# Decoder layer of attention, cross mixing and experts: a piece copy moved from ScalarE to GpSimd, batched small columns and inverse deviations, and new instruction orders in the attention

## The chip, the cores and the metric

One core of a Trainium2 chip runs the whole program in one launch. The metric is the device time of that core in microseconds (us); the runs before have a median of 232.91.

## The reference

The input x is 16 batches of 128 rows by 128 columns, ctx the same. Three sublayers follow one another, each closed by a layer norm of x plus its result:

```python
x = _layernorm(x + attention(x, w_qkv, w_out, b_out))        # 16 heads of 8, rotary positions, softmax
x = _layernorm(x + cross(x, ctx, ctx, Wq, bq, Wout, bout))   # FFT correlation, mean over batch and head, top 11 lags, rolls of v
x = _layernorm(x + experts(x, Wg, bg, W1, b1, W2, b2, gamma, beta))  # 8 experts of width 256, 2 chosen per row
```

All is float32. The change touches the first sublayer and what the kernel computes beside it.

## The kernel before, in words

Each engine has its own list of steps, written out one call after another, and semaphores order them between engines; an engine never looks past a step that waits. So the order of the calls in each engine's block is the schedule.

**The attention, batch by batch (n = 0 to 15).** TensorE: `qkv(n)` multiplies x by the projections (L965, with 8 cross columns of x and, L966, 8 of ctx). ScalarE: `keep_qkv(n)` copies it to SBUF (L706). Rotary positions: `rope_products` (L432, L438) and `rope_sum` (L444), on VectorE for batches 0 and 1 and on GpSimd from 2 on; the result is `qk`. For float32 accuracy from bf16 matmuls, q and k are split into three bf16 pieces laid side by side in `stack` (two buffers): `first_piece` (ScalarE, L719) writes the highest piece; `remainder` (VectorE for 0 and 1, then GpSimd, L450) writes `rest`, what it leaves; `second_piece` (ScalarE, L723) and `second_copy` (ScalarE, L727) both round `rest` into `stack`, at two places of it, since the middle piece stands twice on each side; `third_piece` (GpSimd, L456) writes the lowest. `k_transposes(n)` on TensorE turns the k half (L1003), `kT_copy(n)` on ScalarE keeps it (L732). The q half is turned by TensorE for batches 0 to 2 and by SyncE's `q_transpose(n)`, a DMA transpose (L341), from 3 on.

`scores(n, u)`, u = 0 and 1 (L981): 8 matmuls into `score_pair`; `maxima(n, u)` on VectorE (L1383) reduces them to row maxima, `pieces_of_maxima` (L463, L465) splits these, `maxima_transpose(n)` on TensorE (L1028) turns them, `mT_copy(n)` on ScalarE (L745) keeps them and `spread_maxima(n)` in SyncE's queue sends them by two DMAs (L348) into rows of `qT`, so that `scoresT(n, u)` (L997) has the transposed scores less their maxima. `softmax_exp(n, u)` on ScalarE (L737) makes the probabilities; `weighted(n, u)` (L1042, L1046) multiplies v and ones by them. VectorE: `reciprocal` (L1394) and `divide` (L1399); TensorE: `project(n)` (L1059); VectorE: `residual_sum` (L1406), `statistics_of_rows`, `mean_and_variance`, `normal_rows` (L469), for which GpSimd gives the inverse deviation (L493 an addition, L496 a power of -0.5). `residual(g)` (L1413) adds the output bias to four batches of x.

SyncE's queue issues, in order, `spread_maxima(n)`, a background load (among them the expert weights w1 and w2, from n = 6 on), `q_transpose(n + 3)`, and so on; `q_transpose(n)` waits for `third_piece(n)` and `second_copy(n)`.

**Around the loop.** For k = 8 to 15 every list is a loop whose body handles several batches at once, shifted: TensorE has `scoresT(k-6, 0)`, `scores(k-4, 0)`, `qkv(k)`, `project(k-7)`, `scoresT(k-6, 1)`, `scores(k-4, 1)`, the two halves of `weighted(k-6)`, `k_transposes(k-2)`, `maxima_transpose(k-4)`. Ahead of it a start and behind it a drain are written out. `keep_clock(i)` is i matmuls whose result nobody reads (L945, L951), where TensorE would wait.

**Beside and behind the attention.** `w1_high_piece(i)` on ScalarE (L702) and `w1_low_piece(i)` on GpSimd (L521), i = 0 to 3, split the expert weights into two parts each. Behind the last exponential, ScalarE loads a function table, runs `key_spectrum` and takes the last deviation (L846). VectorE then makes products of spectra (L1561), and `part` and `lag` by two TENSOR_SCALAR and two SCALAR_TENSOR_TENSOR (L1565 to L1571), whose inputs are in SBUF. These go through a matmul, a top 11 and a softmax, in series, before the cross result. GpSimd's `add_cross_bias(g)` (L601) works on four batches each. The experts, from about 114 us to the end, are not touched.

## Time and profile before

| what | us |
|---|---|
| median of 3 runs | 232.91 |
| lowest, highest | 232.44, 234.08 |
| profiled execution, span from its first to its last instruction | 229.2 |
| TensorE busy in it | 215.3 (94%) |
| VectorE | 181.3 (79%) |
| ScalarE | 142.5 (62%) |
| GpSimd | 111.6 (49%) |

The page gives no whole time for the profiled execution, only its span; what lies around the span is in the runs' times alone. A row of a timeline gives start and duration in us; `x8` is the number of instructions merged in it, and a bracket the idle time of the engine before it and what ended that. PE is TensorE's matmuls, PEld its weight loads, DVE VectorE, ACT ScalarE, POOL GpSimd, SPq SyncE's DMA issues. The granted clock of TensorE is 0.991 of full speed on the mean over the span, and 1.00 throughout the attention.

### The profile page before, as it was taken

To read this page: it belongs to the slowest core of one execution; us is meant where nothing else is said; L and a number is where in the kernel's file an instruction comes from. 1 tells how busy PE (TensorE), PEld (TensorE's weight loads), DVE (VectorE), ACT (ScalarE), POOL (GpSimd) and SP (SyncE) were. 2 spreads that over 40 slices of the span, in tenths; PEclk is the share of its full clock that TensorE was granted. 3 is DMA by queue.
4 is the path that set the end of the run, shared out by engine and by line. 5 is a ranking of instruction groups with operands and counts; after the bars stand their busy time and mean duration, and the time that the engine had idled before them with its cause. 6 is when DMAs were issued, how large, how long until landed. Compare 5 with 4: busy or idle time off the path is not lost.

```text
span 229.2 us, 7210 instructions
## 1 busy us (share of the span) xinstructions
PE 215.3 (94%) x2724; PEld 184.4 (80%) x2724; DVE 181.3 (79%) x622; ACT 142.5 (62%) x248; POOL 111.6 (49%) x219
## 2 busy tenths in 40 slices
PE   8989899999999989999999999999999999999970
PEld 7766677778777667778887999789988999889970
DVE  0589998999899899776755779897798868875885
ACT  2488899999999995674489300991029610596112
POOL 5089889999889995513630400252002600040484
PEclk9999999999999999999999999999999999999996
DMA  5951534765569941000000000001000100001001
GB/s 149 286 124 34 106 61 51 171 133 119 138 125 156 156 90 19 14 3 1 3 0 0 3 0 1 0 3 46 4 0 0 46 3 1 0 4 46 1 16 34
DMA packets 32455, 12.32 MB, mean 54 GB/s; under 512 B 19907, under 2 KB 32291, under 8 KB 32419
## 3 DMA queue, kind: packets, MB, share of 16 engines
q1 hardware_dynamic: 31554, 11.48, 24.5%
q8 instruction: 22, 0.36, 0.7%
q10 hardware_dynamic: 864, 0.36, 0.6%
q14 instruction: 15, 0.11, 0.2%
HBM read 6.33 MB, written 1.05 MB: 32 GB/s over the span
## 4 chain that ended last, share of the span: by engine, by line
PE 81%; DVE 6%; DMA 5%; ACT 3%; issue 2%; SPq 1%; DVEq 0%; ACTq 0%
PE bank L1326 13%; PE scoreT_pair L1326 12%; PE score_pair L1298 11%; PE scoreT_pair L1298 8%; PE bank L1042 6%; PE bank L1046 5%; DMA qT_all<-mT 5%; PE bank L965 4%; PE scoreT_pair L997 4%; PE bank L1003 3%; PE score_pair L981 3%; PE scoreT_pair L945 2%; PE bank L1059 2%; ACT early L737 2%; PE bank L940 1%
## 5 line engine op out<-in xcount | busy, mean ns | idle before, releaser
L1383 DVE TENSOR_REDUCE rowmax<-score_pair 128x8 f32<-128x1024 f32 x32 | 39.0, 1218 | 3.3 <-PE score_pair L981 2.0
L608 POOL TENSOR_TENSOR ve<-mv,table 128x4 f32<-128x4 f32 (+1 forms) x12 | 3.3, 277 | 78.1 <-DVE mv L1743 60.2
L737 ACT ACTIVATE early<-scoreT_pair 128x1024 f32<-128x1024 f32 x32 | 32.9, 1027 | 6.0 <-PE scoreT_pair L997 5.9
L1326 PE MATMUL bank<-w,early 128*128 128x128 f32 x256 | 30.1, 276 | 0.0
L1326 PE MATMUL scoreT_pair<-w,early 128*128 128x128 f32 x256 | 29.9, 275 | 0.0
L1326 PEld LDWEIGHTS bank<-w,early 128*128 128x128 f32 x256 | 29.5, 192 | 0.3
L1326 PEld LDWEIGHTS scoreT_pair<-w,early 128*128 128x128 f32 x256 | 29.2, 192 | 0.0
L1298 PE MATMUL score_pair<-x2T_part,w_part 128*128 128x512 f32 x108 | 28.4, 397 | 0.0
L880 ACT ACTIVATE early<-score_pair,b 128x512 f32<-128x512 f32 x38 | 26.0, 691 | 3.2 <-PE score_pair L1298 2.6
L1042 PE MATMUL bank<-early,v_pad 128*32 128x128 f32 x512 | 26.5, 279 | 0.4 <-DVE attnT L1399 0.3
L1046 PE MATMUL bank<-early,head_ones 128*32 128x128 f32 x512 | 25.8, 273 | 0.0
L1298 PEld LDWEIGHTS score_pair<-x2T_part,w_part 128*128 128x128 f32 x108 | 19.6, 188 | 4.9 <-ACT early L880 1.4
L1298 PE MATMUL scoreT_pair<-x2T_part,w_part 128*128 128x512 f32 x78 | 19.9, 391 | 0.0
L1394 DVE RECIPROCAL rden<-bank 128x128 f32<-128x128 f32 x16 | 15.3, 956 | 4.2 <-PE bank L1046 4.1
L880 ACT ACTIVATE early<-scoreT_pair,b 128x512 f32<-128x512 f32 x26 | 17.6, 690 | 0.0
L1298 PEld LDWEIGHTS scoreT_pair<-x2T_part,w_part 128*128 128x128 f32 x78 | 14.6, 188 | 3.0
L732 ACT ACTIVATE kT_all<-bank 128x1024 bf16<-128x1024 bf16 x16 | 16.3, 1020 | 0.2 <-PE bank L1003 0.2
L1042 PEld LDWEIGHTS bank<-early,v_pad 128*32 128x32 f32 x512 | 12.7, 109 | 4.5 <-ACT early L737 1.4
L1046 PEld LDWEIGHTS bank<-early,head_ones 128*32 128x32 f32 x512 | 15.4, 110 | 0.0
L1731 DVE SCALAR_TENSOR_TENSOR x_ext<-bank,gate,x_ext 128x128 f32<-128x128 f32 x32 | 11.1, 346 | 4.7 <-PE bank L1326 4.7
L997 PE MATMUL scoreT_pair<-qT_all,kT_all 64*128 64x128 bf16 x256 | 12.7, 218 | 1.8 <-ACT early L737 0.7
L1731 DVE SCALAR_TENSOR_TENSOR x_ext<-scoreT_pair,gate,x_ext 128x128 f32<-128x128 f32 x32 | 11.1, 346 | 4.0 <-PE scoreT_pair L1326 3.7
(229 smaller groups left out, 474.0 us busy)
## 6 DMA issues: line engine op xcount, KB each, us to landing
w<-in_w SPq DMA_DIRECT2D x8, 256.0 KB, 3.8
x_ext<-in_x SPq DMA_DIRECT2D x4, 256.0 KB, 5.4
qT_all<-mT SPq DMA_DIRECT2D x32, 32.0 KB, 2.3
early<-in_xT SPq DMA_DIRECT2D x3, 256.0 KB, 4.5
early<-in_ctxT SPq DMA_DIRECT2D x3, 256.0 KB, 5.1
out<-qkv_all SPq DMA_DIRECT2D x3, 256.0 KB, 2.3
table<-in_tables SPq DMA_DIRECT2D x1, 321.0 KB
qT_all<-stack SPq DMA_TRANSPOSE x13, 3.4
```

The source lines that it names most:

```text
L732: act.activation(kT[n % DEEP][:, :, :], turned_slots, ACT.Copy).then_inc(s["k_T"], 1)
L737: act.activation(prob[n % 2][:, 2 * u:2 * u + 2, :, :], scoreT_pair[:, :].rearrange("p (i j s) -> p i j s", i=2, j=QUAD), ACT.Exp, scale=S ...
L880: act.activation(hT[:, c, :], hidden_bank(g, c)[:, :], ACT.Relu, bias=b1[:, c:c + 1])\
L965: pe.matmul(qkv_bank[:, 0:3 * D + XC], xT[:, n, :], wqkv[:, :], start=True, stop=True)
L997: mm = pe.matmul(scoreT_pair[:, (QUAD * side + j) * S:(QUAD * side + j + 1) * S], kT[n % DEEP][rows, 2 * j + u, :], qT[n % DEEP][rows, 2 * ...
L1042: pe.matmul(sum_bank(n)[WIDE * j:WIDE * (j + 1), 0:S], v_pad[n % 2][:, j, i, :], prob[n % 2][:, i, j, :], start=(i == 0), stop=(i == QUAD ...
L1046: mm = pe.matmul(sum_bank(n)[WIDE * j:WIDE * (j + 1), S:2 * S], head_ones[:, i * WIDE:(i + 1) * WIDE], prob[n % 2][:, i, j, :], start=Fals ...
L1298: mm = pe.matmul(hidden_bank(g, c)[:, :], w1_part[:, w, c * P:(c + 1) * P], x2T_part[:, x, :], start=(k == 0), stop=(k == 2))
L1326: mm = pe.matmul(expert_bank[k % 4][:, e4 * D:(e4 + 1) * D], hT[:, f, n * P:(n + 1) * P], w2[:, f, :], start=(c == 0), stop=(c == CH - 1))
L1383: dve.tensor_reduce(rowmax[:, H // 2 * u:H // 2 * (u + 1)], score_pair[:, :].rearrange("p (r t) -> p r t", t=S), AX_X, ALU.max).then_inc(s ...
L1394: dve.reciprocal(rden[:, :], sum_bank(n)[:, S:2 * S]).then_inc(s["rden_ready"], 1)
L1731: dve.scalar_tensor_tensor(total, product, weight, total, ALU.mult, ALU.add).then_inc(s["summed"], 1)
```

## The change

`second_copy(n)` for n from 2 to 15 goes from ScalarE's list to GpSimd's. `small_columns`, which adds the cross biases to 16 columns of one batch, handles four batches at once. `inverse_deviation(n)` becomes `inverse_deviations(n, end)`, for two batches in most calls; its tables hold `DEEP` = 4 batches in one tensor. In all four engine lists of the attention the loop is gone and every step is written out in a new order; SyncE's list is the same.

```diff
-        mv1 = [sb(f"mv1{i}", [P, 2]) for i in range(DEEP)]
-        ve1 = sb("ve1", [P, 1])
-        rs1 = [sb(f"rs1{i}", [P, 1]) for i in range(DEEP)]
+        mv1_all = sb("mv1_all", [P, DEEP, 2])
+        mv1 = [mv1_all[:, i, :] for i in range(DEEP)]
+        ve1 = sb("ve1", [P, 2])
+        rs1_all = sb("rs1_all", [P, DEEP])
+        rs1 = [rs1_all[:, i:i + 1] for i in range(DEEP)]
...
+            def inverse_deviations(n, end):
+                at, wide = n % DEEP, end - n
+                pool.wait_ge(s["y1_aggr"], end)
+                wait(pool, s["rs1_ready"], n)
+                pool.tensor_tensor(ve1[:, 0:wide], mv1_all[:, at:at + wide, 1], tab("eps")[:, 0:wide], ALU.add).then_inc(s["ve1_ready"], wide)
+                pool.wait_ge(s["ve1_ready"], end)
+                wait(pool, s["x1_ready"], end - DEEP)
+                pool.tensor_tensor(rs1_all[:, at:at + wide], ve1[:, 0:wide], tab("minus_half")[:, 0:wide], ALU.pow)\
+                    .then_inc(s["rs1_ready"], wide)
+
+            def second_copy(n):
+                pool.wait_ge(s["rest_ready"], n + 1)
+                pool.tensor_copy(piece(n, 5 * HD, 5 * HD), heads(rest[:, :])).then_inc(s["mid_copy"], 1)
...
-                pool.wait_ge(s["qkv_kept"], n + 1)
-                pool.tensor_tensor(x_ext[:, n, D:D + 2 * XC], qkv_all[:, n, 3 * D:QKV], small_b[:, :], ALU.add)\
+                pool.wait_ge(s["qkv_kept"], GT * (g + 1))
+                at = slice(GT * g, GT * (g + 1))
+                pool.tensor_tensor(x_ext[:, at, D:D + 2 * XC], qkv_all[:, at, 3 * D:QKV], small_b[:, :].unsqueeze(1).broadcast_to([P, GT, 2 * XC]),
+                                   ALU.add).then_inc(s["xe_ready"], 1)
```

The parts of the new lists that the prediction speaks of, each engine's calls in their order:

```
VectorE, start:  rope_sum(1) keep_turned third_piece(0) remainder(1) qT_copy(0) residual(0) third_piece(1) maxima(0,0)
         before: rope_sum(1) third_piece(0) residual(0) remainder(1) qT_copy(0) keep_turned third_piece(1) maxima(0,0)
TensorE, start:  qkv(0) keep_clock(3) keep_clock(3) qkv(1) turn_projection qkv(2) keep_clock(2) keep_clock(2) qkv(3)
         then:   scores(1,1) qkv(6) scores(2,0) maxima_transpose(1) scoresT(0,0) k_transposes(3) scores(2,1) scoresT(0,1)
         before: scores(1,1) qkv(6) keep_clock(2) scoresT(0,0) scores(2,0) maxima_transpose(1) k_transposes(3) scoresT(0,1)
ScalarE, start:  keep_qkv(5) mT_copy(0) second_piece(3) kT_copy(2) first_piece(4) mT_copy(1) softmax_exp(0,0)
GpSimd,  start:  rope_sum(3) third_piece(2) second_copy(2) rope_products(4) remainder(3) rope_sum(4) second_copy(3) third_piece(3)
TensorE, a turn: scores(6,0) scoresT(4,0) maxima_transpose(5) qkv(10) project(3) k_transposes(7) scoresT(4,1) scores(6,1)
                 weighted(4,0) weighted(4,1)
         next:   scoresT(5,0) scores(7,0) qkv(11) maxima_transpose(6) k_transposes(8) scoresT(5,1) scores(7,1) project(4)
                 weighted(5,0) weighted(5,1) scores(8,0) scoresT(6,0)
         (the one ahead of scoresT(8,0) has maxima_transpose(8) behind qkv(13) likewise)
ScalarE, a turn: mT_copy(5) softmax_exp(4,0) keep_qkv(10) second_piece(8) softmax_exp(4,1) kT_copy(7) first_piece(9)
TensorE, drain:  scoresT(10,0) keep_clock_late(2) k_transposes(13) scoresT(10,1) ... weighted(11,0) k_transposes(15) scores(14,0)
                 weighted(11,1) ... scores(14,1) scoresT(12,0) project(10) keep_clock_late(1) scoresT(12,1) scores(15,0)
ScalarE, drain:  w1_high_piece(0) keep_qkv(15) softmax_exp(9,1) kT_copy(12) first_piece(14) mT_copy(11) softmax_exp(10,0) kT_copy(13)
                 ... softmax_exp(11,1) kT_copy(15) w1_high_piece(1) mT_copy(13) softmax_exp(12,0) softmax_exp(12,1)
         before: ... softmax_exp(11,1) w1_high_piece(0 to 3) mT_copy(13) softmax_exp(12,0) kT_copy(15) softmax_exp(12,1)
         end:    softmax_exp(15,1) w1_high_piece(2) w1_high_piece(3) function_table key_spectrum
GpSimd,  end:    ... w1_low_piece(0) w1_low_piece(1) pad_v(14) pad_v(15) inverse_deviations(10,12) inverse_deviations(12,14)
                 inverse_deviations(14,15) w1_low_piece(2) w1_low_piece(3) add_cross_bias(0)
```

## Rows read from the trace of the kernel before

**Rows 1.** The page's part 4: the chain that ended last, by engine.
```profile
PE 81%; DVE 6%; DMA 5%; ACT 3%; issue 2%; SPq 1%; DVEq 0%; ACTq 0%
```

**Rows 2.** Busy time of each engine in one stretch of 5 us, core 0.
```profile
50.00:55.00 5.00, 5.00 (x113) 3.93 (x111) 4.59 (x11) 4.77 (x9) 4.54 (x11) 1.00 0.54 121
```

**Rows 3.** TensorE's weight loads in order of time: start us, us, line, operation, count.
```profile
53.19 0.23 PEld L997 LDWEIGHTS scoreT_pair<-qT_all,kT_all 64*128 64x128 bf16 x8
...
53.74 0.30 PEld L965 LDWEIGHTS bank<-wqkv,early 128*128 128x128 f32 x2
...
54.62 0.30 PEld L1059 LDWEIGHTS bank<-wo,attnT 128*128 128x128 f32 x2
...
56.57 0.16 PEld L1042 LDWEIGHTS bank<-early,v_pad 128*32 128x32 f32 x8 [0.15 <-ACT early L737]
...
58.19 0.23 PEld L997 LDWEIGHTS scoreT_pair<-qT_all,kT_all 64*128 64x128 bf16 x8
```

**Rows 4.** ScalarE in order of time, between two exponentials of one turn.
```profile
54.86 0.41 ACT L727 ACTIVATE stack<-rest 128x256 bf16<-128x256 f32 x1
55.49 1.03 ACT L737 ACTIVATE early<-scoreT_pair 128x1024 f32<-128x1024 f32 x1 [0.23 <-PE scoreT_pair L997]
```

**Rows 5.** GpSimd's groups, shapes apart: count | busy us, mean ns.
```profile
L456 POOL TENSOR_TENSOR stack<-rest,stack 128x256 bf16<-128x256 f32 x14 | 9.8, 702 | 0.0
...
L610 POOL TENSOR_TENSOR rs<-ve,table 128x4 f32<-128x4 f32 x9 | 9.1, 1014 | 0.7
L496 POOL TENSOR_TENSOR rs<-ve,table 128x1 f32<-128x1 f32 x15 | 8.5, 569 | 1.2
...
L506 POOL COPY v_pad<-qkv_all 128x128 f32<-128x128 f32 x16 | 4.9, 307 | 7.4 <-ACT qkv_all L706 4.5 <-PE bank L1046 3.0
...
L529 POOL COPY early<-x_ext 128x512 f32<-128x512 f32 x4 | 2.3, 619 | 0.0
```

**Rows 6.** The chain in order of time, at the start.
```profile
12.46 0.76 DVE x_ext L1413
13.22 0.55 DVE rest L450
...
14.12 1.01 ACT kT_all L732
...
24.38 0.60 SPq L348
...
25.02 3.10 DMA qT_all<-mT
```

**Rows 7.** Issues of the maxima's DMA (L348): time from issue to landing.
```profile
DMA to landing us min/median/max: 2.1/2.3/3.2
```

**Rows 8.** The chain in the drain, and VectorE's maxima(14, 1) from its timeline.
```profile
84.62 1.07 ACT kT_all L732
...
86.22 0.33 PE score_pair L981 x8
...
84.12 1.16 DVE L1383 TENSOR_REDUCE rowmax<-score_pair 128x8 f32<-128x1024 f32 x1
```

**Rows 9.** GpSimd in order of time.
```profile
82.21 3.73 POOL L521 TENSOR_TENSOR w_part<-w,w_part 128x512 fp32r<-128x512 f32 x3 [0.47 <-ACT w_part L702]
...
101.25 0.55 POOL L496 TENSOR_TENSOR rs<-ve,table 128x1 f32<-128x1 f32 x1
```

**Rows 10.** VectorE in order of time.
```profile
81.55 0.23 DVE L463 CAST mstack<-rowmax 128x16 bf16<-128x16 f32 x1
...
85.39 0.59 DVE L463 CAST mstack<-rowmax 128x16 bf16<-128x16 f32 x1
...
104.69 0.34 DVE L1568 SCALAR_TENSOR_TENSOR lag<-table,reim,part 65x128 f32<-65x128 f32 x1
```

**Rows 11.** ScalarE's w1_high group (count | busy, mean), and its timeline at the end.
```profile
L702 ACT ACTIVATE w_part<-w 128x512 fp32r<-128x512 f32 x4 | 2.2, 647 | 0.0
...
102.01 0.30 ACT L846 ACTIVATE sd<-mv,table 128x1 f32<-128x1 f32 x1 [0.78 <-DVE mv L1424]
```

More of the change, by code:

```diff
@@ new lines, in _ @@
+            kT_copy(10)
+            keep_qkv(13)
+            first_piece(12)
+            mT_copy(9)
+            softmax_exp(8, 0)
+            second_piece(12)
+            keep_qkv(14)
+            softmax_exp(8, 1)
+            kT_copy(11)
+            first_piece(13)
+            softmax_exp(9, 0)
+            mT_copy(10)
+            second_piece(13)
+            w1_high_piece(0)
+            keep_qkv(15)
+            softmax_exp(9, 1)
+            kT_copy(12)
+            first_piece(14)
@@ L810, in _ @@
+            mT_copy(11)
             softmax_exp(10, 0)
+            kT_copy(13)
             second_piece(14)
-            second_copy(14)
-            kT_copy(13)
             softmax_exp(10, 1)
@@ L1158, in _ @@
             weighted(1, 1)
+            scores(4, 0)
+            scoresT(2, 0)
+            maxima_transpose(3)
+            qkv(8)
             k_transposes(5)
[L1160 to L1171 removed]
+            project(1)
@@ new lines, in _ @@
+            scoresT(2, 1)
+            scores(4, 1)
+            weighted(2, 0)
+            weighted(2, 1)
+            scoresT(3, 0)
+            scores(5, 0)
+            maxima_transpose(4)
+            k_transposes(6)
+            qkv(9)
+            project(2)
+            scoresT(3, 1)
+            scores(5, 1)
+            weighted(3, 0)
+            weighted(3, 1)
+            scores(6, 0)
+            scoresT(4, 0)
+            maxima_transpose(5)
+            qkv(10)
+            project(3)
@@ new lines, in _ @@
+            k_transposes(7)
+            scoresT(4, 1)
+            scores(6, 1)
+            weighted(4, 0)
+            weighted(4, 1)
+            scoresT(5, 0)
+            scores(7, 0)
+            qkv(11)
+            maxima_transpose(6)
+            k_transposes(8)
+            scoresT(5, 1)
+            scores(7, 1)
+            project(4)
+            weighted(5, 0)
+            weighted(5, 1)
+            scores(8, 0)
+            scoresT(6, 0)
+            maxima_transpose(7)
+            k_transposes(9)
@@ new lines, in _ @@
+            qkv(12)
+            scoresT(6, 1)
+            scores(8, 1)
+            project(5)
+            weighted(6, 0)
+            weighted(6, 1)
+            scoresT(7, 0)
+            scores(9, 0)
+            qkv(13)
+            maxima_transpose(8)
+            k_transposes(10)
+            scoresT(7, 1)
+            scores(9, 1)
+            project(6)
+            weighted(7, 0)
+            weighted(7, 1)
+            scores(10, 0)
+            scoresT(8, 0)
+            maxima_transpose(9)
@@ new lines, in _ @@
+            qkv(14)
+            k_transposes(11)
+            scoresT(8, 1)
+            scores(10, 1)
+            project(7)
+            weighted(8, 0)
+            weighted(8, 1)
+            scoresT(9, 0)
+            scores(11, 0)
+            maxima_transpose(10)
+            k_transposes(12)
+            qkv(15)
+            project(8)
+            scoresT(9, 1)
+            scores(11, 1)
+            weighted(9, 0)
+            weighted(9, 1)
+            scores(12, 0)
+            maxima_transpose(11)
```

380 lines of the change are left out of this document (243 added, 137 removed).

## The prediction

> **What bounds the kernel now.** First the chain that ended last, as shares [rows 1]: TensorE holds 81% of the span, all other engines together under a tenth. Then a stretch of the loop [rows 2]: in 5.00 us TensorE is busy 5.00, ScalarE 4.77, VectorE 4.59, GpSimd 4.54. A busy TensorE can hide waits, so third the weight loads, which show when each step starts [rows 3]. One turn is scoresT(n, 0) at 53.19 to the next at 58.19: 5.00 us per batch, eight turns from batch 2 to batch 10. In it TensorE waits for ScalarE once, 0.15 us, for the second exponential; everything else is its own steps end to end. Fourth ScalarE in the same turn [rows 4]: both piece copies stand between the two exponentials, the second one takes 0.41, and still ScalarE is idle 0.23 until TensorE has the next scores. So the copy that leaves ScalarE delays nobody in the loop. The whole gain open there is 0.15 per turn, and exp(n, 1) stands behind scoresT(n, 1) in the new order too, with scores and weighted(n, 0) beside it. I take 0 for the loop from shorter waits; the bounds are -1.2 (8 x 0.15) and +0.8 (0.1 a turn for steps that follow one another in another order).
>
> Where does TensorE wait? At the two ends. At the start for the first keys and for the maxima's DMA [rows 6], in the drain for kT_copy(15) and for the same DMA [rows 8]. These are what the new order can give.
>
> **Second copy to GpSimd.** Nearest rows [rows 5]: a GpSimd COPY of 128x128 takes 0.31, of 128x512 0.62, so 256 columns about 0.41, of which 0.3 to 0.4 is occupancy; the upper bound is an operation of two inputs on 256 columns, about 0.7. Removed from ScalarE: 14 x 0.41 of work [rows 4]. Added to GpSimd: 0.4 per turn. In return the inverse deviations come in pairs: a power of one column takes 0.57, of four 1.01 [rows 5], so of two about 0.71, that is 0.36 a batch in place of 0.57, and the addition ahead of it is halved as well. The sixteen small column sums become four. Together some 0.4 saved a turn, so GpSimd stays near its 4.54 of 5.00 [rows 2] and the loop's turn hides all of it. If the cover went (copy at 0.7), GpSimd would need 4.85, still under 5.00. But rest, which the copy reads, is now freed by GpSimd, and third_piece stands before or behind the copy in its queue: k_transposes and the queue's q_transpose(n) wait for both. In the loop I find them done over 3 us before they are asked for.
>
> **The start.** On VectorE residual(0) (0.76 on the chain, from 12.46) stood ahead of remainder(1) (13.22), and behind it hang second_piece(1), kT_copy(0) at 14.12 and the first scores [rows 6]. In the new order remainder(1) comes first, so it can start once first_piece(1) is there. Against this an added keep_clock(3) stands ahead of qkv(1) and delays it by about 0.7, but keep_qkv(2) and second_piece(0) come as late as before, so it is swallowed down to 0.2. kT_copy(0) then starts near 13.7 and all follows 0.4 earlier. Next, mT_copy(0) goes ahead of kT_copy(2) and second_piece(3), and scores(2, 0) and maxima_transpose(1) are issued ahead of scoresT(0, 0), which waits for the DMA anyway: maxima(1) are turned near 22.3. The second spread then waits in SyncE's queue for q_transpose(3), no longer for ScalarE. GpSimd's rope_sum(4), second_copy(3) and third_piece(3), some 1.8 us behind remainder(3), end near 21.9 by my count; the transpose's issue of 1.3 puts the spread at 23.25, where it was at 24.38 before; with the 3.1 us that it took to land [rows 6] scoresT(1, 0) starts at 27.1 (23.25 + 0.65 + 3.1 + 0.05), not 28.16. I take -1.1 (bounds -1.9, the maxima's transpose alone deciding, and 0).
>
> **The maxima's way in the loop.** This is the added wait that I fear. From maxima_transpose(n) on TensorE to scoresT(n, 0): transpose and mT_copy to its end 0.56, SyncE's first issue 0.64, then the landing of the second, 2.1 to 3.2 with a median of 2.3 [rows 7], and 0.05: 3.4 to 4.5 us. Before, it had one turn and 0.2, that is 5.2 [rows 3]. In the new order the transpose stands behind scoresT(n-1, 0) in most turns, which leaves 4.4 to 4.7; for n = 6 and n = 8 it stands behind scoresT, scores and qkv, 0.55 + 0.88 = 1.43 after the turn's start [rows 3], which leaves 5.0 + 0.2 - 1.4 = 3.8. Beside the weight loads the landing is in the upper half of its range, so I take 0.2 at each of these two, +0.4 together (bounds 0 and 2 x 0.7). Queued behind a late scoresT is all of TensorE, and there is no second copy of that time anywhere.
>
> **The drain.** Before, kT_copy(15) ran at 84.62 to 85.7, behind four w1_high_piece and an exponential, and scores(15, 0) waited for it until 86.2 [rows 8]. Now k_transposes(15) and kT_copy(15) come earlier, and only w1_high_piece(1) stays in that stretch. VectorE's maxima(14, 1), which ended at 85.3 [rows 8], then becomes what scores(15, 0) waits for, about 0.7 earlier. Of this 0.2 is given back, since k_transposes(13), one more w1_high_piece and first_piece(14) ahead of mT_copy(11) come into the drain's first turns. What is behind scores(15, 0), down to the last weighted, is TensorE's own pace with the maxima's DMA [rows 8] 0.4 to 0.5 earlier. I take -0.5 (bounds -1.2 and +0.5).
>
> **The tail.** w1_high_piece(2) and (3), 0.65 each [rows 11], now stand behind the last exponential, ahead of the table load and key_spectrum. ScalarE waited 0.78 us for the last variance there [rows 11] and about as long for its work before: the 1.2 fits, with some 0.3 left. They release w1_low_piece(2) and (3) on GpSimd only after inverse_deviations(14, 15), which ended at 101.8 [rows 9]: 2 x 1.24 to about 104.3, and add_cross_bias(0) of the same size behind them to 105.5. Until now GpSimd was idle when VectorE did its two SCALAR_TENSOR_TENSOR on table and part at 104.69 [rows 10], which read two SBUF tensors. What such a meeting costs: a CAST of rowmax took 0.23 at 81.55, and 0.59 at 85.39, with GpSimd inside the w1_low pieces [rows 10, 9]; it ended when that piece did. By that, the first of the two waits from 104.69 to 105.55 less what of its 0.34 runs beside it: +0.7 on the path (lag, correlation, top k, all in series). Bounds 0, if VectorE slips in between two GpSimd operations, and 1.3, a whole one.
>
> The Trainium skill (SBUF — State Buffer, section "SBUF: two separate sides") speaks against this move: VectorE and GpSimd share a port pair as an exclusive lock held for a whole instruction, taken by VectorE for two SBUF inputs or a two-port mode. The CAST's end at GpSimd's end agrees. The page would let the two TENSOR_SCALAR ahead of the sums block as well, and the tail would then lose 1.3 where I take 0.7.
>
> **The sum.** -1.1 + 0.4 - 0.5 + 0.7 = -0.5 us. The page gives 229.2 us of span for the profiled execution and no whole time; the runs' median of 232.91 is 3.7 more, for what lies around the span, which the change does not touch. So 228.7 of span, and 232.4 us. A measurement of this kernel tells some 1% (2.3 us) from no change; by that the forecast is no change.
>
> **Rivals.**
> *R1, the ends give all they can (faster).* The landings stay at the median 2.3, nothing waits in the loop and half of the 0.15 per turn goes, the drain gives 1.2, VectorE is not blocked: -1.1 - 0.6 - 1.2 = -2.9, 230.0 us. For it: ScalarE has 0.3 a turn more room. Against: TensorE has no room to use it [rows 2, 3].
> *R2, the maxima's DMA takes the place of the scores as the loop's bound (slower).* Place: scoresT(n, 0) of batches 3 to 10. Price: a way of 1.25 + L against 4.4, so it decides from a landing L of 3.15; where mT_copy also stands behind another ScalarE step of 0.4, from 2.75. With 0.4 in eight turns and 0.7 in two of them: 3.8, less 0.5 + 1.1, plus 0.7: +2.9, 235.8 us. For it: 3.2 occurs [rows 7]. Against: the median of 2.3.
> *R3, the change does not balance as it says:* GpSimd with a copy of 0.7 delays the pieces at the start, where its queue is the longest one, and the gain of the start is gone: +0.6, 233.5 us.
> *R4, as forecast, but VectorE is not blocked in the tail:* 231.7 us.
>
> **How the numbers follow.** Forecast 0.42, R4 0.15, R1 0.20, R2 0.15, R3 0.08. Faster by over 1% is R1 alone: 0.20. Slower by over 1% needs 235.2, R2: 0.15. Between them 0.65. The range of 8 in 10 leaves out the further half of R1 and of R2: 229.8 to 235.3.
>
> **What would show it.** Right: turns of 5.00 (4.95 to 5.05) from batch 2 to 10 with ScalarE idle more than before between the exponentials; scoresT(1, 0) at 27.1; waits of TensorE on the maxima's DMA in front of scoresT(6, 0) and scoresT(8, 0), 0.1 to 0.5; scores(15, 0) some 1.1 earlier than 86.2; the two SCALAR_TENSOR_TENSOR of the lag starting or ending with a GpSimd operation. Wrong: turns of 4.8 or less; TensorE waiting for third_piece or the copy of GpSimd; a lag that is done as soon after the last variance as before; a GpSimd copy above 0.5.

## The result, and the profile of the changed kernel

The changed kernel takes 237.0 us (median of 4 runs, 236.46 to 238.1), the kernel before 233.5 in the runs beside it: ratio 1.020, 95% interval 1.015 to 1.025. A second set (run `after_again` below, 6 runs of this and 11 of before) gives 1.022 (1.016 to 1.027). The forecast was 232.4, no change, in a range up to 235.3; the result lies above it, on the side of R2.

Page part 4 of the changed kernel's first profiled execution (chain by engine; it answers to [rows 1]):

```profile
PE 72%; DVE 11%; DMA 9%; issue 3%; SPq 2%; ACT 2%; DVEq 0%; ACTq 0%
```

TensorE's share of the chain has gone from 81% to 72%, VectorE's from 6 to 11, DMA's from 5 to 9. The windows view says the same of the loop. The columns are the stretch, its length, then busy us with instructions of PE, PEld, DVE, ACT and POOL, granted clock, DMA share, GB/s. First before, then changed (second profile), both from 33.20, at which scoresT(2, 0) has just begun:

```profile
33.20:73.00 39.80, 39.80 (x887) 31.34 (x887) 36.41 (x80) 37.94 (x64) 36.52 (x81) 1.00 0.63 130
```
```profile
33.20:73.00 39.80, 38.32 (x844) 30.39 (x844) 35.97 (x73) 35.15 (x55) 34.44 (x70) 1.00 0.69 117
```

Before, TensorE is busy 39.80 of 39.80. After, it starts 844 matmuls in the time of 887, and all four engines are less busy: none of them is the new bound, and they wait for each other. The granted clock is 1.00 in both, so it has no part in this.

**Stages.** The first weight load of a step marks its start (as in [rows 3]). Start: of scoresT(0, 0). Fill: from there to scoresT(2, 0). Loop: the eight turns to scoresT(10, 0). Drain: to the last weights of weighted(15, 1). Tail: to the first weights of the lag product. Rest: to the end of the span. All in us, of the profiled executions:

| kernel | ratio to before (95%) | start | fill | loop | drain | tail | rest |
|---|---|---|---|---|---|---|---|
| before | 1 | 22.7 | 10.5 | 40.0 | 25.3 | 6.9 | 123.9 |
| changed, first profile | 1.020 (1.015 to 1.025) | 25.1 | 10.6 | 42.0 | 26.1 | 8.3 | 124.1 |
| changed, after_again | 1.022 (1.016 to 1.027) | 22.6 | 10.6 | 42.1 | 25.8 | 8.3 | 124.2 |
| a_start | 1.026 (1.020 to 1.032) | 22.9 | 10.6 | 42.8 | 25.7 | 8.6 | 124.8 |
| a_tail | 1.017 (1.011 to 1.023) | 25.4 | 10.6 | 42.4 | 26.7 | 6.8 | 124.1 |
| a_max | 1.024 (1.018 to 1.030) | 22.4 | 10.6 | 43.0 | 25.9 | 8.3 | 124.1 |
| a_ktr | 1.020 (1.014 to 1.027) | 22.5 | 10.6 | 42.6 | 27.3 | 8.3 | 125.1 |
| a_mt | 1.022 (1.017 to 1.026) | 23.2 | 10.6 | 42.0 | 26.0 | 8.7 | 124.6 |
| a_three | 1.015 (1.009 to 1.020) | 24.7 | 10.6 | 43.0 | 26.7 | 6.8 | 124.1 |
| a_act | 1.012 (1.004 to 1.020) | 25.1 | 9.7 | 43.0 | 27.4 | 8.3 | 125.3 |
| a_pe | 1.050 (1.044 to 1.057) | 22.3 | 12.1 | 44.4 | 28.9 | 8.3 | 124.1 |
| b_pool | 1.000 (0.996 to 1.004) | 24.8 | 11.1 | 40.3 | 25.7 | 6.9 | 123.9 |
| b_group2 | 1.002 (1.000 to 1.005) | 22.9 | 10.8 | 40.0 | 26.3 | 6.9 | 124.1 |
| b_group | 1.030 (1.023 to 1.038) | 22.8 | 15.6 | 43.7 | 25.7 | 6.9 | 124.1 |
| b_help | 1.088 (1.078 to 1.097) | 24.7 | 15.6 | 56.9 | 28.2 | 6.9 | 124.1 |
| b_one | 1.002 (0.999 to 1.006) | 22.8 | 10.5 | 41.1 | 25.5 | 6.9 | 123.8 |
| b_max | 1.022 (1.016 to 1.028) | 22.1 | 10.6 | 45.0 | 26.8 | 6.9 | 123.8 |
| b_late | 1.021 (1.015 to 1.027) | 22.4 | 10.9 | 43.8 | 27.0 | 6.9 | 123.8 |
| b_tail | 1.009 (1.006 to 1.012) | 22.7 | 11.1 | 40.4 | 25.2 | 8.7 | 123.9 |

(a_ is the changed kernel with an edit, b_ the kernel before with one.) Every stage is read from one profile. TensorE's granted clock is 1.00 in fill, loop, drain and tail of all of them but these, whose times contain what the clock cost: the drain of a_act, a_ktr and a_pe (0.94), the tail of a_act, a_ktr, a_start and a_mt (0.94, 0.93, 0.89, 0.87), fill and loop of b_group (0.91), and fill, loop and drain of b_help (0.91, 0.84, 0.88).

One profile differs from the next also where the kernel doesn't. The loop of the changed orders took 42.0 and 42.1 in the two profiles of the unedited kernel, 42.8 and 42.4 in a_start and a_tail, whose edits lie outside it; that of the old orders took 40.0 to 40.4 in before, b_pool, b_group2 and b_tail. So a difference of 2 us in the loop is clear of this, one of 0.5 is not.

Between before and after_again the difference of 4.4 us is start and fill 0, loop +2.1, drain +0.5, tail +1.4, rest +0.3. The rest goes with the grouped steps: it is 124.1 or 124.2 in all profiles that have them and the full clock around the tail, 123.8 or 123.9 in all without them. The start of 25 instead of 22.7 is no part of the change: TensorE got its full clock later, see the end.

### The profile page after: what moved, and what is told of

Its sections match the earlier page's. It is cut to its first block, busy times and chain, and to the rows that moved or that the text cites. A ratio compares the mean times of both kernels' runs of the same rounds, so it can differ in the third digit from the quotient of the medians.

```text
span 236.2 us, 7175 instructions
## 1 busy us (share of the span) xinstructions
PE 217.7 (92%) x2724; PEld 186.5 (79%) x2724; DVE 186.6 (79%) x622; ACT 140.5 (59%) x234; POOL 111.1 (47%) x207
## 3 DMA queue, kind: packets, MB, share of 16 engines
q1 hardware_dynamic: 31554, 11.48, 24.7%
## 4 chain that ended last, share of the span: by engine, by line
PE 72%; DVE 11%; DMA 9%; issue 3%; SPq 2%; ACT 2%; DVEq 0%; ACTq 0%
PE bank L1489 12%; PE scoreT_pair L1489 12%; PE score_pair L1461 11%; PE scoreT_pair L1461 8%; DMA qT_all<-mT 7%; PE bank L1136 4%; PE bank L1059 3%; PE scoreT_pair L1091 3%; PE bank L1140 3%; PE scoreT_pair L1039 3%; DVE rowmax L1546 3%; SPq L350 2%; PE score_pair L1075 2%; PE bank L1097 2%; DMA qT_all<-stack 2%
## 5 line engine op out<-in xcount | busy, mean ns | idle before, releaser
L1136 PE MATMUL bank<-early,v_pad 128*32 128x128 f32 x512 | 26.3, 277 | 0.5 <-DVE attnT L1562 0.3
L1140 PE MATMUL bank<-early,head_ones 128*32 128x128 f32 x512 | 25.8, 273 | 0.0
L1136 PEld LDWEIGHTS bank<-early,v_pad 128*32 128x32 f32 x512 | 13.2, 109 | 3.8 <-ACT early L789 0.9
L1954 DVE SCALAR_TENSOR_TENSOR x_ext<-bank,gate,x_ext 128x128 f32<-128x128 f32 x32 | 11.1, 346 | 5.0 <-PE bank L1489 5.0
L1075 PE MATMUL score_pair<-kT_all,qT_all 48*128 48x128 bf16 x256 | 12.8, 217 | 2.5 <-DVE rowmax L1546 0.9
```

Of the source, the lines that this page charges most:

```text
L1075: mm = pe.matmul(score_pair[:, (QUAD * side + j) * S:(QUAD * side + j + 1) * S], qT[n % DEEP][rows, 2 * j + u, :], kT[n % DEEP][rows, 2 * ...
L1136: pe.matmul(sum_bank(n)[WIDE * j:WIDE * (j + 1), 0:S], v_pad[n % 2][:, j, i, :], prob[n % 2][:, i, j, :], start=(i == 0), stop=(i == QUAD ...
L1140: mm = pe.matmul(sum_bank(n)[WIDE * j:WIDE * (j + 1), S:2 * S], head_ones[:, i * WIDE:(i + 1) * WIDE], prob[n % 2][:, i, j, :], start=Fals ...
L1954: dve.scalar_tensor_tensor(total, product, weight, total, ALU.mult, ALU.add).then_inc(s["summed"], 1)
```

## The experiments

### The changed kernel again, and one suspected loss taken out at a time

> The changed kernel once more, unedited, beside the three below on one chip. If the 4.3 us by which its profiled run went beyond its own fastest timed runs were variation, the median stays at 236.5 to 237.5 and the profiled span falls to about 235; scoresT(0,0), at 25.14 us in its first profile, then starts nearer 24. If the start is late by the kernel itself, it is 25 again.

Measured: 236.3 us, scoresT(0, 0) at 22.59. The late start of the first profile was variation of the run, and the last section shows of what.

```diff
 qkv(0)
 keep_clock(3)
-keep_clock(3)
 qkv(1)
+keep_clock(3)
```

> The changed kernel with its second group of three idle matmuls back behind the projection of batch 1. Theory that the start loses by these: qkv(1) comes 0.5 to 1.2 us earlier, scoresT(0,0) as well, and the time falls by 0.5 to 1.5 us against the changed kernel. Rival, that the projection of batch 1 isn't what the later start hangs on (the spread of the maxima of batch 0 behind GpSimd's and ScalarE's work is): under 0.3 us, with scoresT(0,0) where it was.

Measured: scoresT(0, 0) at 22.88, the ratio not lower (1.026, 1.020 to 1.032). That looks like the rival, but the two profiles don't start alike: qkv(1) came at 7.43, later than the 7.31 of after_again, since TensorE had its full clock from 6.2 us on here and from 4.5 there. Beside a_mt, which has all twelve idle instructions and the full clock from 6.0 on, a_start is 0.3 earlier (22.88 against 23.19). So the idle matmuls do cost about 0.3; the total time is too coarse to show it.

```diff
 softmax_exp(12, 1)           # ScalarE
+w1_high_piece(2)
+w1_high_piece(3)
...
 w1_low_piece(1)              # GpSimd
+w1_low_piece(2)
 pad_v(14)
+w1_low_piece(3)
...
 inverse_deviations(14, 15)
-w1_low_piece(2)
-w1_low_piece(3)
```

> The changed kernel with the last two high and the last two low pieces of w1 cast before the last two batches of the attention instead of behind them, so that GpSimd makes no long cast while VectorE normalizes the last rows of x1. Theory that GpSimd's cast holds up VectorE's scale-and-shift: the two that took 1.22 and 1.30 us go back to 0.34 and 0.54, the stretch from weighted(15,1) to the lag product falls from 8.8 to 7.4, the time by 1.4 us, if the pieces don't hold up the drain, where they now lie (then 0.5 to 1 of it comes back there). Rival, that the stretch is long by the order of VectorE's and TensorE's work: no change.

Measured: the tail goes from 8.3 to 6.8, the drain is 0.6 to 0.9 longer, the ratio is 1.017 (1.011 to 1.023), which overlaps the changed kernel's. The tail's loss is w1's pieces; taken out of the tail, about half of it comes back in the drain. The opposite edit on the kernel before (pieces 2 and 3 behind all else on both engines):

> The kernel before with the last two high and low pieces of w1 cast behind everything else of the attention, as the changed kernel has them. By the theory of the blocked VectorE the stretch from weighted(15,1) to the lag product goes from 6.85 to 8.2 to 8.4 us and the time up by 1.0 to 1.4, less what the drain gains by two casts fewer (up to 0.5). Rival, that in this order VectorE is elsewhere when the casts run: 6.9 and no change.

Measured: ratio 1.009 (2.0 us); tail 8.7, 1.9 longer, drain 0.1 shorter. The two edits move the tail by 1.4 and 1.9 us in opposite directions, so its cause is shown. Here is how it looks, GpSimd and VectorE of after_again (start, duration):

```profile
104.45 2.48 POOL L530 TENSOR_TENSOR w_part<-w,w_part 128x512 fp32r<-128x512 f32 x2
107.11 1.27 POOL L653 TENSOR_TENSOR x_all<-x_all,bias 128x512 f32<-128x512 f32 x1 [0.17 <-DVE x_all L1775]
```
```profile
104.58 1.22 DVE L471 TENSOR_SCALAR x_all<-y,mv_all,rs_all 128x136 f32<-128x136 f32 x1
105.72 0.15 DVE L1772 RECIPROCAL rs_all<-sd 128x1 f32<-128x1 f32 x1
105.91 1.30 DVE L1775 TENSOR_SCALAR x_all<-y,mv_all,rs_all 128x8 f32<-128x8 f32 x2
...
108.78 0.34 DVE L1791 SCALAR_TENSOR_TENSOR lag<-table,reim,part 65x128 f32<-65x128 f32 x1
109.04 0.34 DVE L1794 SCALAR_TENSOR_TENSOR lag<-table,reim,part 65x128 f32<-65x128 f32 x1
```

Normal for L471 is 0.35 and for the pair of L1775 0.54. Each waits for one of GpSimd's two pieces (1.24 us) to end; the reciprocal between them does not. The two SCALAR_TENSOR_TENSOR that the prediction named run free: add_cross_bias (L653) has ended at 108.38.

### The maxima's way, in the changed orders

```diff
 weighted(2, 1)               # TensorE, batches 4 to 11
+maxima_transpose(4)
 scoresT(3, 0)
 scores(5, 0)
-maxima_transpose(4)
...
+mT_copy(4)                   # ScalarE, batches 4, 6, 8, 10
 softmax_exp(3, 0)
-mT_copy(4)
```

> The changed kernel with the transpose of the maxima of batches 4 to 11 on TensorE back right behind the weighted sums, ahead of the transposed scores, and their copy on ScalarE ahead of the exponential. Theory that the loop loses by the maxima's way by DMA: the waits for it (2.6 us over batches 5 to 10) go, the eight turns come down from 42.0 to 40.0 to 40.5, the time by 1.5 to 2 us. Rival, that the turns are long by other work (VectorE's busy time is up by 5 us, GpSimd's long queue, the q transposes' landing 4.1 us instead of 3.4): the waits go over to another name and the time falls by less than 0.5.

Measured: no wait of TensorE for the DMA is listed in the loop any more (after_again has 1.6 us of them, the first profile of the changed kernel 2.6), and the loop is 43.0, no shorter than 42.1. TensorE's waits from 33.2 to 73:

```profile
PEld bank L1122 <- DVE mstack L467: 3.0, 5, 0.8
PEld bank L1122 <- issue: 0.5, 2, 0.3
PEld bank L1136 <- ACT early L789: 0.3, 2, 0.2
PEld scoreT_pair L1091 <- issue: 0.2, 1, 0.2
```

The transpose, asked for earlier, waits for VectorE. With k_transposes(m + 2) ahead of maxima_transpose(m) as well:

> The changed kernel with early maxima once more, and the transposes of k ahead of them, so that VectorE has TensorE's 0.5 us of k more to finish the maxima's rows before they are asked for. By the theory that TensorE, busy all the time, loses each wait: the 3.0 us of waits for VectorE go and the eight turns come from 43.0 to 40.5 to 41. Rival, that the stretch only moves on to the next wait (ScalarE's k copy, GpSimd's third piece): 42 or more.

Measured: loop 42.6; the rival. And the changed kernel with ScalarE's edit, and TensorE's maxima 6 and 8 ahead of qkv:

> The changed kernel, and in the turns of batches 4, 6, 8 and 10 alone ScalarE copies the turned maxima ahead of the exponential (1.03 us) instead of behind it, with the transpose of 6 and 8 ahead of the projection; the rest of TensorE's order stays. In those four turns the spread left 1.66 to 2.02 us after the turn's start, in the others 0.9. Theory that ScalarE's exponential ahead of the copy is what made the spread late: the four spreads leave at 0.9 to 1.0, the waits for the DMA in front of the four transposed scores go, and the loop comes from 42.1 to 41 or less. Rival, that the exponential, now behind the copy and waiting for it, costs TensorE as much at the second half: 42 or more.

Measured: the spread leaves 1.1 to 1.2 us after the turn's start for batches 4, 6 and 10, not 1.7 to 2.0, but 1.8 for batch 8, and the loop is 42.0, as without the edit; the rival. TensorE still waits 2.0 us for the DMA, in front of scoresT(5, 0), (8, 0) and (9, 0): 0.33, 0.31 and 1.33. Two of these three spreads had left 0.9 us after the turn's start, so the exponential ahead of the copy is not what their waits come from. All three edits (idle matmuls back, w1's pieces out of the tail, maxima early) at once:

> The changed kernel with all three edits tried one by one (idle matmuls back, w1's casts ahead of the tail, maxima early). If the losses are separate and add, the tail is 6.9, the drain and loop some 69 us together, and the time 1 us below the changed kernel. If the orders as a whole are the loss, the loop is still 42 or more, and the time stays over 1% above before.

Measured: ratio 1.015 (1.009 to 1.020), with an interval that overlaps the changed kernel's. By the stages the tail is 1.4 shorter, loop and drain are 69.6 together, 1.6 longer than in after_again. The three suspected losses do not add up to the whole: the orders as a whole keep the loop at 42 or more in each variant.

### The work that moved, without the new orders

```diff
+second_copy(n)               # GpSimd, ahead of third_piece(n), n = 2 to 15
 third_piece(pool, n)
...
 second_piece(n)              # ScalarE
-second_copy(n)
```

> The kernel before with nothing changed but the second copy, which GpSimd makes ahead of the third piece, every step's order kept. Its 0.40 us comes on top of some 4.6 us of GpSimd's work in a turn of 5.00, and leaves 0.6 to 0.8 of ScalarE's 4.8. Theory that GpSimd's queue in the loop has room: the eight turns stay at 40.0, the time within 0.5 us of before. Rival, that GpSimd becomes a bound of the loop: turns of 5.1 to 5.3, the time 1 to 3 us above before.

Measured: ratio 1.000 (0.996 to 1.004), loop 40.3 with seven turns of 5.00 and one of 5.23. The move costs nothing and gives nothing. ScalarE's waits from 33.2 to 73, b_pool:

```profile
ACT early L803 <- PE scoreT_pair L1104: 4.2, 8, 0.5
```

That is where the 0.41 per turn went: ScalarE waits for TensorE 0.5 a turn, where it waited 0.23 [rows 4].

> All that the change does to GpSimd's work (second copy, cross columns by four batches, inverse deviations by two), with the orders of the kernel before on all four engines. Theory that the loss lies in the orders: the eight turns stay at 40.0 to 40.3 and the time within 0.7 us of before, so 3.5 us or more below the changed kernel. Rival, that the loss lies in the moved work itself: loop 1 to 2 us longer here too.

Measured: ratio 1.088. VectorE waited for the grouped results (deviations 5.1 us, cross columns 4.9 in the stretch), since a group is ready only with its last batch. With each group where it is due, and VectorE's rows 2i and 2i+1 normalized in one turn:

> All that the change does to GpSimd's work, in the orders of the kernel before, and this time with the grouped steps where they are due: cross columns of four batches a turn before the first of them is added, the deviations of two batches once both are there, and VectorE normalizes those two rows together in every second turn. Theory that the moved and grouped work costs nothing and the orders are the whole loss: eight turns of 5.0 (40.0 to 40.4), time within 0.7 us of before, a tail of 6.9. Rival, that grouping itself makes alternate turns of VectorE too full (two rows of 0.34 us each in one): 5.1 to 5.3 in every second turn, time 1 us or more above before.

Measured: ratio 1.030. The other turns were 5.00 to 5.14, one was 8.42, and it starts with one stall; VectorE's wait from 25 to 76:

```profile
DVE y L1568 <- POOL x_ext L524: 4.9, 1, 4.9
```

small_columns(0) stood three steps too late. The stall of 4.9 us cost some 8.7 in fill and loop together, since TensorE, idle meanwhile, then ran at half its clock for 10 us (35.7 to 45.9). Two stretches of this profile, the granted clock stands third from the end:

```profile
34.00:38.00 4.00, 0.00 (x0) 0.00 (x0) 1.81 (x6) 0.00 (x0) 3.04 (x7) 0.71 0.35 68
38.00:42.00 4.00, 3.84 (x27) 2.65 (x29) 2.56 (x6) 1.60 (x3) 0.67 (x1) 0.50 0.12 16
```

Part of b_help's 1.088 is of this kind too (clock 0.84 in its loop). With the call of small_columns(0) moved ahead of pad_v(2):

> The same as the grouped kernel before it, but the cross columns of the first four batches are added ahead of the padding of batch 2's values on GpSimd, where the changed kernel has them, instead of three steps of the rotation later, where VectorE's first residual sum waited 4.9 us for them. By the theory that moved and grouped work costs nothing where it is due: the turn of 8.4 us goes, scoresT(2,0) starts 10.5 to 11.1 us after scoresT(0,0), eight turns of 40.0 to 40.6, and the time is within 0.7 us of before. Rival, that the grouping costs in every second turn: 1 us or more above before.

Measured: ratio 1.002 (1.000 to 1.005), eight turns of 5.00 and 5.01. This kernel has TensorE's and ScalarE's orders of before, and VectorE's but for the paired rows. So all that the change moves and groups costs at most about 1 us in the old orders and nothing in the loop, and the loss of 2% is the orders'. For the drain this doesn't follow: it is 26.3 in this profile, longer than the changed kernel's. The same from the other side:

> The changed kernel's orders with the second copy back on ScalarE, right behind the second piece. What it tells: how much the orders lose without the move. If the orders alone are the loss, the eight turns are 42 to 43 and the time is 3.5 to 5.5 us above before. If GpSimd's long queue under these orders is the loss, the turns come down to 40.5 and the time to within 2.5 us of before (the tail's 1.4 us stays in both).

Measured: loop 43.0, ratio 1.012 (1.004 to 1.020). The loop is no shorter than the changed kernel's own, so GpSimd's longer queue isn't what stretches it. The ratio is below the changed kernel's, but the intervals overlap; whether it gains anything stays open.

> The changed kernel with TensorE's order of before, the other three orders as changed. Theory that TensorE's order alone makes the loop slip (scores ahead of transposed scores in some turns, transposes of the maxima late): the eight turns come from 42.1 to 40.5 or less. Rival, that the orders of VectorE and ScalarE, which differ from turn to turn, do it: 42 or more, with waits of TensorE for VectorE or ScalarE.

Measured: ratio 1.050, loop 44.4. TensorE's order of before doesn't fit the other three new ones. The four lists are one plan; a run with one of them exchanged can't price it.

### A late maxima in the old orders

```diff
-maxima_transpose(m)          # TensorE, m = 4 to 11
 scoresT(m - 1, 0)
 scores(m + 1, 0)
+maxima_transpose(m)
...
-mT_copy(m)                   # ScalarE
 softmax_exp(m - 1, 0)
+mT_copy(m)
```

> The kernel before with one edit in the loop: the transpose of the maxima of batches 5 to 11 behind the first halves of the next turn's transposed scores and scores on TensorE, their copy behind the exponential on ScalarE (in batch 4's turn one place likewise), as the changed kernel has them. Theory that this lateness is what stretches the changed loop: the spread leaves some 0.8 us later, waits for the DMA show up, the eight turns go to 41 to 42. Rival, that a DMA that leaves a turn ahead is still hidden in a loop with equal turns: 40.0 to 40.4 and a time within 0.7 us of before.

Measured: loop 45.0, ratio 1.022 (1.016 to 1.028): this edit alone costs as much as the whole change. It goes further than the changed kernel, though: here ScalarE's copy stands behind the exponential in all eight turns, there in those of batches 4, 6, 8 and 10 only. The chain of waits from 59 to 67, b_max, in order of time, one full turn of it:

```profile
59.62 0.42 PE scoreT_pair L1052 x8
...
60.06 0.02 ACT early L737
60.08 0.37 issue
60.45 0.02 ACTq L85
60.47 0.51 issue
60.98 0.28 ACT mT L745
...
61.28 0.60 SPq L348
...
61.93 3.83 DMA qT_all<-mT
...
65.81 0.42 PE scoreT_pair L1052 x8
```

This is a ring: scoresT(m-1, 0), the exponential (0.94 from 60.04 to 60.98), the copy of the maxima, the issue, the landing, scoresT(m, 0). Each scoresT starts the work that the next one waits for. One round is 65.81 - 59.62 = 6.2 us. No engine of the ring is full; it is long by latency. In the kernel before, the copy and its transpose stand ahead of scoresT(m-1, 0) and its exponential, so this DMA never waits for the DMA of the batch before.

For batch 8 alone:

> The kernel before with the maxima's transpose late for batch 8 alone. If a late spread costs once what it is late, one turn is 5.2 to 5.6, the others 5.0, and the eight come to 40.2 to 40.6. If the loop is a closed chain in which the lost time comes back a turn or two later by the q transposes, which stand behind the spread on SP's queue, the turns after it are longer too and the sum is 41 or more.

Measured: the turns 5.0, then 5.19 and 5.85, then 5.0; loop 41.1. It is paid once, 1.04 us, and nothing comes back later: one late batch closes no ring. The wait in that turn:

```profile
63.77 0.10 PEld L1083 LDWEIGHTS bank<-ident,mstack 128*128 128x128 bf16 x1
64.38 0.23 PEld L1052 LDWEIGHTS scoreT_pair<-qT_all,kT_all 64*128 64x128 bf16 x8 [0.52 <-DMA qT_all<-mT]
```

With the transposes of k behind the maxima too:

> As the run with the late maxima, and the transposes of k behind them too, so that each turn on TensorE has the sequence of a typical turn of the changed kernel (transposed scores, scores, maxima, k, projection), but every turn alike, and VectorE's and GpSimd's orders those of before. Theory that the arrangement inside a turn costs: 41 to 43 for the eight turns. Rival, that what costs is that the changed kernel's turns differ from each other (4.65 to 6.26 us): turns of 5.0 to 5.1.

Measured: loop 43.8 with turns of 4.4 to 5.9, ratio 1.021. Neither side as put: the same list in every turn gave unequal turns and did not save the loop, and the late maxima without this edit had cost no less (45.0).

And b_max with the loads of w1 and w2 out of the loop:

> As the run with the late maxima, but the loads of w1 and w2, which SP issues behind the spreads of batches 6 to 11, are all issued behind those of 12 and 13; read is the loop alone, since the drain now waits for w1. With the late maxima the time from the spread's issue to the transposed scores that waited for it was 3.6 to 3.7 us for batches 4 to 6 and 3.8 to 4.75 for 7 to 10. Theory that the weight loads lengthen the landing: 3.6 to 3.7 for all, and the eight turns come from 45.0 to 43.5 or less. Rival, that the q transposes next to the spreads do it: the later batches stay at 3.8 to 4.7, the loop at 44.5 to 45.

Measured in one run: loop 43.7, at a granted clock of 1.00. The whole took 243.6 us against 231.1, since the drain waits for w1 as expected (33.9, at a clock of 0.85). From the first issue of the spread to scoresT it is 3.6 us for batches 4 to 7, and 3.95, 4.3 and 4.3 for 8 to 10. So the loop is 1.3 us shorter without the weight loads, by one profile each; the spreads of 8 to 10 stay long without them, and why is open.

## Why the prediction was wrong, point by point

**What bounds the kernel.** Right: TensorE, end to end in the loop, and nothing to gain there. What it didn't draw from that row is the other half: with TensorE at 39.80 of 39.80, each wait that an order brings is lost. "I take 0 for the loop from shorter waits", with +0.8 as the bound for steps that follow one another in another order, is the first step that failed: the loop lost 2.1, and without any wait for the DMA (a_max) it was still 3.0 above before.

**Second copy to GpSimd, about 0.41.** Right, and the groups too. GpSimd's groups of after_again, busy us and mean ns:

```profile
L505 POOL CAST stack<-rest 128x256 bf16<-128x256 f32 x14 | 5.6, 401 | 0.0
L500 POOL TENSOR_TENSOR rs_all<-ve,table 128x2 f32<-128x2 f32 (+1 forms) x8 | 5.5, 686 | 1.0
```

The copy takes 0.40 (0.41 forecast), the power of two columns 0.69 (0.71); b_pool and b_group2 show the whole at no cost in the loop. R3's mechanism fell with it, though the gain of the start is gone as R3 has it.

**The start, -1.1.** The steps came in part. kT_copy(0) starts at 13.01 (forecast 13.7, before 14.12) and the first spread is issued at 19.20 (before 19.66), but scoresT(0, 0) starts at 22.59 (22.69): maxima_transpose(1), which now stands ahead of it, waited 0.51 for VectorE until 22.43. The second spread is issued at 23.59 (forecast 23.25, before 24.38), scoresT(1, 0) starts at 27.67 (27.1, 28.16). The rest is given back before scoresT(2, 0), at 33.22 against 33.17, by VectorE, which is on the chain there. after_again:

```profile
25.36 1.08 DVE L1576 TENSOR_TENSOR x_ext<-x_ext,bias 128x512 f32<-128x512 f32 x1
26.37 0.71 DVE L465 CAST mstack<-rowmax 128x16 bf16<-128x16 f32 x1
...
27.20 1.25 DVE L1576 TENSOR_TENSOR x_ext<-x_ext,bias 128x512 f32<-128x512 f32 x1
```
```profile
27.67 0.23 PEld L1091 LDWEIGHTS scoreT_pair<-qT_all,kT_all 64*128 64x128 bf16 x8 [0.81 <-DMA qT_all<-mT]
...
30.82 0.23 PEld L1075 LDWEIGHTS score_pair<-kT_all,qT_all 48*128 48x128 bf16 x8 [0.76 <-DVE rowmax L1546]
```

residual(3) now stands ahead of the maxima that scores(3, 1) waits for, and residuals and casts take up to 0.5 longer beside GpSimd. The failed step is "all follows 0.4 earlier": the 0.4 was lost to a transpose put ahead of scoresT(0, 0), and the forecast stopped at scoresT(1, 0) and didn't ask what is late next. The 0.2 for keep_clock(3) is about right (0.3 between a_start and a_mt). And before and after_again don't start quite alike: the full clock came at 6.4 us in before and at 4.5 in after_again. With the full clock from 6.0 on, as in a_mt, the changed start has scoresT(0, 0) at 23.19, 0.5 later than before. So no gain of the start is hidden in the 0; a small loss may be.

**The maxima's way in the loop, +0.4.** This step failed; the loop lost 2.1. The kind of wait was right. The place was right once: waits of 0.1 to 0.5 were forecast in front of scoresT(6, 0) and (8, 0), and none elsewhere. after_again has these three in the loop:

```profile
48.25 0.23 PEld L1091 LDWEIGHTS scoreT_pair<-qT_all,kT_all 64*128 64x128 bf16 x8 [0.59 <-DMA qT_all<-mT]
...
64.37 0.23 PEld L1091 LDWEIGHTS scoreT_pair<-qT_all,kT_all 64*128 64x128 bf16 x8 [0.31 <-DMA qT_all<-mT]
...
69.56 0.23 PEld L1091 LDWEIGHTS scoreT_pair<-qT_all,kT_all 64*128 64x128 bf16 x8 [0.68 <-DMA qT_all<-mT]
```

They are scoresT(5, 0), (8, 0) and (9, 0). The first profile has five, in front of batches 5, 7, 8, 9 and 10 (0.66, 0.29, 0.33, 0.93, 0.39); batch 6 waits in neither. The way of the DMA to the first of them, after_again, chain from 43.60:

```profile
43.60 0.17 PE bank L1122
43.80 0.29 ACT mT L797
44.10 0.61 SPq L350
44.72 0.04 issue
44.76 3.45 DMA qT_all<-mT
48.21 0.05 issue
48.26 0.40 PE scoreT_pair L1091 x8
```

The term that was mis-sized is the landing. 2.3 was the median of all 32 issues [rows 7], and the median is still 2.2 in after_again and 2.3 in b_max. But TensorE waits for the slow ones: on the chain of the loop they took 3.45 and 3.55 in after_again, 2.65, 3.06, 3.44 and 3.37 in the first profile, and 3.53, 3.83, 2.69 and 4.05 in b_max. The row for it stood in [rows 6], 3.10, and was used for the start alone.

A second thing was overlooked: the forecast counted "transpose and mT_copy to its end 0.56" in all turns, while for batches 4, 6, 8 and 10 the new list has the exponential of 1.02 ahead of mT_copy. The spread leaves 1.66 to 2.02 us after the turn's start for these four, 0.91 to 0.95 for 3, 5, 7 and 9. But most of the waiting isn't there: batches 5, 7 and 9, whose spreads left early, have 1.27 of the 1.58 us in after_again and 1.88 of the 2.60 in the first profile, and a_mt, with ScalarE's order mended, kept its loop of 42.0.

R2 was the nearest rival, with 235.8 against 236.3 and 237.0, and partly by luck: of its sum the loop's 3.8 was 2.1, and the 1.6 that it took off for start and drain was a loss of 0.5. Its own condition (a landing over 3.15, or 2.75 with ScalarE behind another step) was met by most of the landings above. Its price for the loop is of the size that the old orders show, 1.0 for one batch, 3.8 in b_late and 5.0 in b_max.

But R2 isn't all. The turns of after_again are 4.65, 5.29, 5.09, 5.11, 4.75, 6.26, 5.19 and 5.80. TensorE's waits for the DMA are 1.6 us in it and 2.6 in the first profile, and the loops are 42.1 and 42.0 all the same; a_max, which takes these waits out, isn't shorter. It looks as if two ways of about the same length run side by side, through the DMA and through VectorE, and removing one leaves the other; no run takes out both, so this is argued from the chains, not shown. From 67 us on the chain of after_again runs through VectorE:

```profile
67.52 1.22 DVE rowmax L1546
68.77 0.48 DVE mstack L465
...
69.51 0.28 DVE st L1582
69.80 0.87 DVE rden L1557
...
70.89 0.72 DVE rowmax L1546
...
72.03 0.73 DVE x_all L471 x2
...
73.22 0.29 DVE y L1569
73.50 0.09 DVE mv_all L1587
73.59 1.12 DVE rowmax L1546
```

Statistics, a reciprocal and normal rows stand between the maxima that TensorE waits for. Which of these positions costs what isn't shown; exchanging single steps of the changed orders left the loop at 42.0 to 43.0 each time. Shown is that the orders together cost it (b_group2 against after_again). Shown is also that late maxima in every turn can cost as much by themselves (b_max), not that they are what costs it in the changed kernel.

**The drain, -0.5.** The sign was wrong: +0.5. scores(15, 0) comes 12.53 us after scoresT(10, 0) (before 12.95), 0.4 earlier where 0.7 less 0.2 was forecast. The size came out, the step did not: maxima(14, 1) had ended at 87.45, and scores(15, 0), at 87.89, came behind scoresT(12, 1), which had waited 0.66 for the exponential until 87.31. The first profile has 12.76, 0.2 earlier. Behind scores(15, 0) 0.9 is lost: the step "TensorE's own pace" failed. VectorE's L467, 0.20 else, meets w1_low_piece(0) and (1) (after_again), and scores(15, 1) waits 0.68 for the maxima behind it:

```profile
87.74 2.50 POOL L530 TENSOR_TENSOR w_part<-w,w_part 128x512 fp32r<-128x512 f32 x2
```
```profile
87.86 1.22 DVE L467 TENSOR_TENSOR mstack<-rowmax,mstack 128x16 bf16<-128x16 f32 x1
```

That the block is the cause of the whole 0.9 is argued from the chain, not shown by a run of its own; and b_group2, with the pieces where they were before, has a drain of 26.3, so one profile of each doesn't settle the drain.

**The tail, +0.7.** The mechanism was right, R4 fell, size and place were off: 1.4, on the scale-and-shift steps ahead of the lag, not on the two sums. The operations that were held up are L471 and L1775, which write normalized rows; the two TENSOR_SCALAR and the two sums on `part` ran at their usual 0.28 and 0.34. The step that failed is the choice of what blocks, and for how long: the 0.7 was made by a CAST that was held up for 0.36 only because GpSimd's piece was nearly done.

The rule in the Trainium skill (SBUF — State Buffer, section "SBUF: two separate sides") was read in the prediction as letting TENSOR_SCALAR block as well, with a loss of 1.3. The trace agrees with that reading: 1.22 in place of 0.35 for L471, and 1.4 for the tail.

**The base.** What lies around the span is 1.8 to 1.9 us in most runs (235.42 less 233.6), not 3.7: the profiled execution of before was one of its fastest, about 231.1. The forecast of 232.4 is the median less 0.5 either way; only the split of the 3.7 was misread.

**The sum.** Forecast -1.1 + 0.4 - 0.5 + 0.7 = -0.5. Measured 0 + 2.1 + 0.5 + 1.4 = 4.0, and 0.3 after the tail. Half of the miss is the loop.

## What to carry to other kernels

Where one engine is busy without a gap, moving a step off another engine gave nothing here (b_pool), and a new order inside such a stretch has only waits to bring; price the order by what stands ahead of each step on every engine's list, not on the busy one's alone. Ask of each DMA with a latency near the length of a turn whether its issue now waits, through any engine's queue, for the DMA of the turn before: closed in every turn, as in b_max, such a ring can set the turn's length, and its latency is to be taken from the chain, from the transfer that is waited for, not from the median of all. When an edit takes a wait out and the time stays, look for what TensorE waits for instead (here VectorE). Long GpSimd operations on SBUF belong where VectorE has nothing urgent.

## What the runs showed of the chip that was not expected

**TensorE gets its full clock at a different time from run to run.** The same twelve idle instructions (a `keep_clock(3)` shows as six), first in the first profile of the changed kernel, then in after_again:

```profile
6.96 2.68 PEld L1039 LDWEIGHTS scoreT_pair<-mean_w 128*128 128x128 f32 x12
```
```profile
5.97 1.42 PEld L1039 LDWEIGHTS scoreT_pair<-mean_w 128*128 128x128 f32 x12
```

0.22 us each against 0.12. The windows view prints a granted clock of 1.00 for these microseconds in both, but the clock record of the trace file has no entry there yet. It begins, with the full clock, at 10.2 us in the first and at 4.5 in the second, and the durations change there. Ahead of it every profile starts alike, with fourteen idle instructions of 0.22 from 1.03 on.

In fourteen of the twenty profiles the record begins at 4.0 to 6.4 us, and scoresT(0, 0) starts at 22.1 to 23.2; in six it begins at 10.1 to 10.7, and scoresT(0, 0) starts at 24.7 to 25.4, under both orders. The late start goes with the late clock in all twenty, and 2 us or more between two spans may be this alone. What decides between early and late isn't shown. With a late clock the six idle instructions more ahead of qkv(1) cost 0.4: 25.1 to 25.4 with twelve there (three profiles), 24.7 to 24.8 with six (three profiles). A stage at the start is to be compared only between profiles whose clock came at the same time.

**A stall of TensorE cost more than itself.** In b_group VectorE stood still for 4.9 us and TensorE's weight loads for 4.7; the clock fell to half at 35.7 and came back at 45.9, and the turn that began at 38.4 took 8.42 us.

**VectorE's small operations pay for GpSimd's large ones.** A TENSOR_TENSOR of 128x16 took 1.22 us in place of 0.20, a TENSOR_SCALAR of 128x136 1.22 in place of 0.35, each until the 1.24 us operation of GpSimd that it met had ended.
